# A two-layer attention kernel: three stops per slot for its plan, values' products two key blocks at a time, six probability buffers, and a new table of places

## What is computed

```python
# layer 0: group norm, 8 heads of 32 channels, projection, residual
h = group_norm(x, 32 groups) * gn_w + gn_b
q, k, v = split(qkv_w @ h + qkv_b)                 # per head 32 x 1024
w = softmax(q^T k / sqrt(32), over keys)           # 8 heads, 1024 x 1024
x = x + proj_w @ (v w^T) + proj_b
# layer 1: one head, q and k of 32 channels, v of 256
x = gamma * (Wv x) softmax((Wq x)^T (Wk x))^T + x  # 1024 x 1024
```

## Time and profile before

| | us |
|---|---|
| median of 3 runs (lowest, highest) | 1744.56 (1738.89, 1748.17) |
| the profiled execution | 1744.39 |
| its span, first to last instruction | 1742.5 |
| prologue | 80.6 |
| first batch | 163.8 |
| loop, six batches | 1227.5 |
| last batch | 176.5 |
| epilogue | 94.1 |

### The profile page before, as it was taken

One profiled execution on the slowest core, in us unless ns is written; L12 is line 12 of the kernel. 1 busy time (PEld: TensorE's weight loads), 2 busy tenths in 40 slices (PEclk: granted clock), 3 DMA queues, 4 the chain that ended last, 5 costly groups with the idle time before them and its releaser, 6 DMA issues.

```text
span 1742.5 us, 25501 instructions
## 1 busy us (share of the span) xinstructions
PE 1589.6 (91%) x7120; PEld 880.3 (51%) x7120; DVE 1129.3 (65%) x1916; ACT 759.2 (44%) x1377; POOL 1201.1 (69%) x560
## 2 busy tenths in 40 slices
PE   3989899999999989999899999999999999999867
PEld 1544444465445744457344664456543574446336
DVE  3776768666677667767576665866677666674233
ACT  2145355444454344553455434544445535454412
POOL 2088587766777587785777767776786758797803
PEclk9599899999999999999899998999999999999979
DMA  5133031301303013120412013030130302200100
GB/s 131 25 98 74 1 76 41 73 5 48 99 19 74 14 53 89 36 52 20 107 40 53 22 50 98 19 74 7 44 99 20 74 13 77 52 1 7 43 19 25
DMA packets 38741, 85.74 MB, mean 49 GB/s; under 512 B 10304, under 2 KB 20416, under 8 KB 38592
## 3 DMA queue, kind: packets, MB, share of 16 engines
q1 hardware_dynamic: 38208, 82.88, 18.9%
q0 software_dynamic: 384, 1.05, 0.3%
HBM read 18.29 MB, written 8.39 MB: 15 GB/s over the span
## 4 chain that ended last, share of the span: by engine, by line
PE 70%; DVE 12%; issue 10%; ACT 4%; POOL 3%; DMA 1%; SPq 1%; DVEq 0%; POOLq 0%; ACTq 0%
PE pv L513 13%; PE st L482 12%; PE pv L491 11%; PE work L555 10%; DVE mpart L825 6%; PE work L612 6%; PE work L575 4%; PE work L619 3%; PE work L587 3%; POOL acc L801 3%; PE st L474 2%; ACT probs L678 1%; PE rec L530 1%; PE work L561 1%; PE work L581 1%
## 5 line engine op out<-in xcount | busy, mean ns | idle before, releaser
L801 POOL TENSOR_TENSOR acc<-acc,probs 128x1024 f32<-128x1024 f32 x384 | 898.7, 2373 | 110.1 <-ACT probs L678 108.8
L678 ACT ACTIVATE probs<-st 128x512 f32<-128x512 f32 x1152 | 618.4, 597 | 618.3 <-PE st L482 477.7
L825 DVE TENSOR_REDUCE mpart<-work 128x1 f32<-128x512 f32 x1024 | 646.0, 680 | 170.7 <-PE work L555 167.5
L555 PE MATMUL work<-ks,qs 96*128 96x512 f32 x1024 | 447.7, 496 | 45.1 <-DVE mpart L825 20.4
L482 PE MATMUL st<-qs,ks 98*128 98x512 f32 x1024 | 371.6, 443 | 26.6 <-ACT probs L678 12.9
L482 PEld LDWEIGHTS st<-qs,ks 98*128 98x128 f32 x1024 | 180.3, 194 | 285.0 <-ACT probs L678 138.2
L801 POOL TENSOR_TENSOR acc<-probs 128x1024 f32<-128x1024 f32 x64 | 151.2, 2372 | 220.3 <-ACT probs L678 220.2
L555 PEld LDWEIGHTS work<-ks,qs 96*128 96x128 f32 x1024 | 198.1, 197 | 207.2 <-DVE mpart L825 105.9
L491 PE MATMUL pv<-probs,vt 128*32 128x512 f32 x2048 | 278.4, 616 | 0.1
L513 PE MATMUL pv<-probs,l_vt 128*128 128x256 f32 x1024 | 246.3, 383 | 3.0 <-ACT raw L736 2.2
L513 PEld LDWEIGHTS pv<-probs,l_vt 128*128 128x128 f32 x1024 | 190.9, 191 | 36.0 <-ACT raw L736 4.9
(11 more groups left out here) (73 smaller groups left out, 937.7 us busy)
## 6 DMA issues: line engine op xcount, KB each, us to landing
qs<-part_hi SPq DMA_DIRECT2D x116, 128.0 KB, 2.4
ks<-part_hi SPq DMA_DIRECT2D x116, 128.0 KB, 2.4
xa<-in_x SPq DMA_DIRECT2D x16, 512.0 KB, 4.0
y<-in_x SPq DMA_DIRECT2D x8, 1024.0 KB, 5.3
out<-raw SPq DMA_DIRECT2D x32, 256.0 KB, 2.2
qs<-part_lo SPq DMA_DIRECT2D x60, 128.0 KB, 2.4
ks<-part_lo SPq DMA_DIRECT2D x60, 128.0 KB, 2.6
qs<-mrow SPq DMA_DIRECT2D x256, 2.0 KB
```

What stands on the lines that cost most here:

```text
L555: last = mm(bank, qs[g][0:HI_HI_LO, j, t0:t0 + P], ks[g][0:HI_HI_LO, j, half * HALF:(half + 1) * HALF], start=True, stop=True)
L678: nc.scalar.activation(probs[:, n % PRING, half * HALF:(half + 1) * HALF], st[:, (2 * n + half) % ST_BANKS, :], ACT.Exp).then_inc(s_exp1 i ...
L801: pool.tensor_tensor(a, first, probs[:, n % PRING, :], ALU.add).then_inc(s_add0, 1)
L825: last = dve.reduce_max(mpart[:, 4 * j + tb, half:half + 1], bank, AX.X)
```

## The change

Each slot has three stops: the plan's table counts 216 stops instead of 72 slots (`STOPS = 3`; stop 3n+k lies in slot n). PE issues the first score matmul of the slot, the entries of stop 0, the second score matmul, the entries of stop 1, then the slot's sums, then a product if one is due, then the entries of stop 2. A product is due in every fourth slot, and takes two key blocks one after the other. The ring of probability buffers has six instead of four. All places in `STEADY` and `MAXIMA_OF_STOP` are new. ACT and DVE walk the same entries in the plan's order; POOL's and SP's programs keep their order.

```diff
+STOPS = 3
-PRING = 4
+PRING = 6
-    "norm": (9, 12, 13, 15, 17, 17, 19, 22, 24, 25, 34, 35),
+    "norm": (32, 33, 34, 40, 52, 53, 60, 72, 88, 112, 118, 119),
...
-    plan = [[] for _ in range(SLOTS)]
+    plan = [[] for _ in range(STOPS * SLOTS)]
...
-            def scores_by_key(n, kind, b):
+            def scores_by_key(n, half, kind, b):
...
-                for n, entries in enumerate(plans[kind]):
-                    entries = [e for e in entries if e[0] not in NO_BANK or e[0] in ("SUM", "SUM1")]
-                    if n in units:
-                        scores_by_key(n, kind, b)
+                for n in range(SLOTS):
+                    stops = [[e for e in plans[kind][STOPS * n + k] if e[0] not in NO_BANK] for k in range(STOPS)]
+                    ready = [e for k in range(STOPS) for e in plans[kind][STOPS * n + k] if e[0] in ("SUM", "SUM1")]
+                    for half in range(2):
+                        if n in units:
+                            scores_by_key(n, half, kind, b)
+                        for e in stops[half]:
+                            fill_bank(e, kind, b)
+                    for e in ready:
+                        fill_rec(e, kind, b)
...
-                        product_l1(n - 2, kind, b, entries)
+                        product_l1(n - 2, kind, b, stops[2])
                         continue
-                    for e in entries:
-                        fill_bank(e, kind, b)
                     if n == 1 and kind not in ("prologue", "first"):
+                        product_l0(SLOTS - 3, b - 1)
                         product_l0(SLOTS - 1, b - 1)
-                    elif n % 2 and n - 3 in units and unit_use(n - 2)[0] == 0:
+                    elif n % 4 == 1 and n - 5 in units and unit_use(n - 2)[0] == 0:
...
+                        product_l0(n - 4, b)
                         product_l0(n - 2, b)
+                    for e in stops[2]:
+                        fill_bank(e, kind, b)
```

More of the change, by code:

```diff
@@ L450, in _ @@
             mm = nc.tensor.matmul
-            def scores_by_key(n, kind, b):
+            def scores_by_key(n, half, kind, b):
                 layer, i = unit_use(n)
[L455 to L480, removed]
-                    j = 2 * pair + half
-                    mm(bank, ks[g][0:ROWS, j, blk * P:(blk + 1) * P], qs[g][0:ROWS, j, c * HALF:(c + 1) * HALF],
-                       start=True, stop=True).then_inc(s_st0, 1)
@@ new lines, in scores_by_key @@
+                at = 2 * n + half
+                before = at - ST_BANKS
+                while kind == "first" and before // 2 in range(L1_AT, L1_AT + L1_UNITS):
+                    before -= ST_BANKS
+                if kind == "epilogue" and before < 2 * L1_AT:
+                    pe.wait_ge(s_exp0, 2 * L0_UNITS * B)
+                elif before >= 0:
+                    wait_exp(pe, before // 2, b, before % 2 + 1)
+                elif kind != "first":
+                    pe.wait_ge(s_exp0, 2 * L0_UNITS * b + before + 1)
@@ new lines, in scores_by_key @@
+                bank = st[:, at % ST_BANKS, :]
+                if layer:
+                    c, part = i // 2, i % 2
+                    if i == half == 0:
+                        pe.wait_ge(s_mrow1, 32 * b)
+                    for q in range(2):
+                        s0 = (4 * part + 2 * half + q) * P
+                        last = mm(bank[:, q * QUARTER:(q + 1) * QUARTER], ks1[0:ROWS, s0:s0 + P],
+                                  qs1[0:ROWS, c * QUARTER:(c + 1) * QUARTER], start=True, stop=True)
+                    last.then_inc(s_st1, 1)
+                    return
@@ L485, in product_l0 @@
+                g, c, blk, pair = i // 32, i // 16 % 2, i % 16 // 2, i % 2
+                if i % 16 == half == 0:
+                    pe.wait_ge(s_mrow[g][c], 128 * b + 128)
+                j = 2 * pair + half
+                mm(bank, ks[g][0:ROWS, j, blk * P:(blk + 1) * P], qs[g][0:ROWS, j, c * HALF:(c + 1) * HALF],
+                   start=True, stop=True).then_inc(s_st0, 1)
             def product_l0(n, b):
@@ L538, in fill_bank @@
             def fill_bank(e, kind, b):
-                if e[0] in ("SUM", "SUM1"):
-                    fill_rec(e, kind, b)
-                    return
                 i = place[kind][e]
@@ L715, in step @@
                 units = slots_of(kind)
-                for n, entries in enumerate(plans[kind]):
+                for n in range(SLOTS):
+                    entries = [e for k in range(STOPS) for e in plans[kind][STOPS * n + k]]
                     if n in units:
```

40 lines of the change are left out of this document (19 added, 21 removed), and 6 rows, old and new, of the table MAXIMA_OF_STOP.

## The result

The changed kernel takes 1616.49 us (median of 4 runs, 1612.85 to 1617.91), the kernel before 1745.26 in the same comparison: a ratio of 0.926, with a 95% interval of 0.923 to 0.929.

The account below looks back on a forecast made before the run. The prediction took PE to bound the kernel, busy for 91% of the span. Its sum 1742.5 - 35.3 - 28.4 - 10 + 2 = 1670.8, plus 1.9 us around the span, gave 1672 us, range 1628 to 1713.

Parts of the forecast that it names:

- (1): Values' products on PE: 118 fewer changes into and out of strips at 0.34 us; 35.3 us off, bounds 9 and 40.
- Rival C: Double products on PE: the second product waits for its weights, leaving 9 us of 40; 1698 us, chance 0.03.
- (2): Maxima matmuls on PE: shorter runs cut the weight loads' wait for DVE from 68.9 to 40.5 us; 28.4 off.
- (3): Transposes of the column maxima on PE: other work ahead of them takes 10 us off a 14.7 us wait.
- (4): Moved places: group 1's first maxima may wait for copies on SP's queue; 2 us added, bounds 0 and 14.
- a wait on a copy: Sign of a wrong forecast: first maxima of group 1 or 0 wait on a copy to the stacks.
- (5): Six probability buffers: part of ACT's 12.6 us wait for POOL could go; counted as nothing.
- 160 groups: Sign of a right forecast: 160 strip groups on PE after joining, where PE went over 278 times before.
- PE's busy time: Sign of a right forecast: PE's busy time falls by some 30 us or more.
- waits for the column maxima near 5: Sign of a right forecast: the loop's wait for the column maxima, 14.7 us before, falls to near 5.
- a wait for DVE that stays at 69 us: Sign of a wrong forecast: the wait for DVE stays at 69 us in spite of shorter runs of maxima.
- Rival B: PE's waits: scores also stop waiting for exponentials, and the maxima's wait goes nearly whole; 1634 us, chance 0.20.

Follow-up runs that it names:

- e17: Kernel before, the group norm's small DVE operations rewritten so none has both operands in SBUF (one in PSUM): 1739.6 us, ratio 0.997.
- e16: Kernel before with three stops alone (old places, single products, ring of four) and the norm rewritten as in e17: 1714.9 us, ratio 0.983 to the kernel before.
- e14: Changed kernel with single products and the norm rewritten as in e17: 1653.5 us, ratio 0.948 to the kernel before.
- e13: Changed kernel with the norm's small DVE operations rewritten so none has both operands in SBUF: 1600.4 us, ratio 0.918 to the kernel before.
- e18: Everything of the change but the new places, with the norm rewritten as in e17: 1742.5 us, ratio 0.997 to the kernel before.
- e10: Kernel before with each slot's entries divided over three stops; old places, single products, ring of four: 1750.6 us, ratio 1.003.
- e7: Kernel before with maxima over 256 of 512 keys and the exponentials' input scaled by 0.0001 (output not the attention's): 1667.1 us, ratio 0.957.
- e9: Changed kernel with single products and a ring of four: 1726.6 us, ratio 0.987 to the kernel before.
- e4: Changed kernel with single products; new places, three stops and ring of six stay: 1711.4 us, ratio 0.980 to the kernel before.
- e12: Changed kernel with two of a batch's four layer-0 sums moved next to a double product: 1632.4 us, ratio 0.934 to the kernel before.
- e6: Kernel before with the new places alone (old order, single products, ring of four): 1862.5 us, ratio 1.068.

## Why the prediction was wrong, by its steps

With nothing held the change can be walked step by step, each a difference of two medians: held operations away 6.3 (to e17), three stops 24.7 (e16), new places and ring 61.4 (e14), joins 53.1 (e13), and the changed kernel's own held operations back, -16.1. That is 129.4, where the sum had 71.7.

(1) **Joined products, 35.3.** The price was right: 160 strip groups, 1.86 us for a double one, and 0.33 us a join by the medians where the sum had 0.34. But taking the joins in measured 53.1 on the new places and -27.6 on the old, ring included (e16 to e18). The price is PE's work; the rest is waits that come or go with it, and why they do is open. Rival C fell with the 1.86 us: the second product's weights, in the same rows, load beside matmuls in flight in each of the 128 blocks. The sentence of the Trainium skill behind it ("TensorE: Matmul & The Clock Gate", Part 3, "The mechanism"), that LDWEIGHTS overlap with matmuls in flight only where the row group differs, isn't borne out here; the same section also has a load pulled ahead when it targets the background weight buffer, and that would fit.

(2) **Three stops, 28.4.** Measured 24.7 once nothing is held, -5 as it stands (e10). The size was near; that an order can move a small operation under POOL's add wasn't in it. The row it was taken from says little: the weight loads' wait fell from 68.9 to 56.7, not to 40.5, while lighter reductions were worth 76 us (e7).

(3) and (4) **Transposes and places moved, 10 and -2.** (4) is the step that failed. The new places and the ring measured 61.4; the ring's part was 15 where it was measured (e9 to e4). Of the transposes' lost time of some 17 us in the loop under 1 is left in the changed kernel; in the step from e16 to e14 it is some 10 of the 61. The copies cost more than the 2 of the sum: PE waited for the stacks of group 0 or 1 once for 7.8 us at the start before, and after for 2.5, 3.0 and 2.8 us more, 8.3 in all, inside the bound of 14; the sign "a wait on a copy" did show, small. What is left, some 40 us (an estimate from these differences), is the places of all other entries. (4) priced the moved entries by the copies alone and the rest at nothing, and (2) backed this with "the number of maxima in a whole slot is as uneven as before (0 to 5), so a backlog that spans slots stays". Per slot it is; per stretch of 16 slots ten DVE operations left slots 16 to 31, in which PE waited for DVE, and went to slots 0 to 15 and 48 to 71. Counting the plan's entries by stretch would have shown this move before any run. That the move is what shortens the stretch is read from the windows, in both orders; no run moved these operations by themselves.

(5) **Ring, nothing.** 15 us with single products (e9 to e4).

The joins' 18 us over their term and the new places' and ring's 53 over theirs make up the difference to 129; three stops (-4) and held operations (-10) go the other way.

Of the signs named beforehand 160 groups, 1.86 us, PE's busy time down by 89 and waits for the column maxima near 5 came true. A batch takes 185.8 us and not 193, and the epilogue 90.3 and not 94. The wait for DVE stayed at 56.7 instead of 40, near the sign "a wait for DVE that stays at 69 us", and yet the time fell further: that row measures weight loads, not PE. Rival B, at 1634, was nearest in size, and still 18 us short; it had the waits of the scores (87.1 to 35.4) going, but its larger part, that the wait of the maxima's weight loads goes nearly whole, did not come.

The rule that would have warned of the held operations is the Trainium skill's, "SBUF — State Buffer", section "SBUF: two separate sides": DVE and GpSimd share a pair of ports as an exclusive lock, and a DVE operation with two SBUF inputs stands until GpSimd's ends, where that one reads SBUF. The trace agrees: 0.16 us alone, 2.27 beside POOL, 0.16 beside POOL with one operand in PSUM. It also shows more than one add waited out: in e10 the held operation starts in one add and ends with the next, after 3.2 us, and in the first batch of the kernel before one stands for 6.03 us, past the ends of two adds and to that of a third.

What stays open: which of the moved entries carry the 61 us, since the table was not taken apart; which waits start it when joins cost 28 us on the old places, with PE's loss in the loop up by some 45 us, up to 20 of it by the clock; and why two sums moved by a few slots cost 16 us (e12) with nothing more held. There the time at the lower clock grows too, from 38 to 51 us, worth 7 us at most.

## What to carry to other kernels

Price a new order by stretches in which one engine waits, not by single slots, and count lost time between starts on the bounding engine; a row on weight loads can stay while the time falls. Look for small operations that take ten times their usual time, and see what runs on the other engine: moving one operand to PSUM was worth 16 us here, and it decided how three experiments on single parts read. Parts of a hand-placed order don't add: three stops alone cost 5 us, joins and ring 18, places 117, and all together gave 129.

## What the runs showed of the hardware

Small DVE operations with both operands in SBUF end with an add of POOL (1.23 and 2.27 us instead of 0.16), also three in a row (e6), and in e10 only with the second (3.2 us). With one of the two operands in PSUM they aren't held (0.16 us beside an add, e13), nor are reductions from PSUM (0.68 us beside POOL and alone) or copies from it (0.15 us). One operation with a single operand, in SBUF, was held once (0.60 us instead of 0.17, first batch of the changed kernel). After PE stood for 3.9 us its granted clock was 0.50 for some 6 us (e4), and a product took 1.94 us instead of 1.06. Going from a strip group to another shows no cost: a second product behind the first takes 0.86 us, where a single one takes 1.00, with its weights loading beside.
